# Routed rows sent to their expert's slots while the attention stage still runs, and PSUM banks exchanged between two uses

## The chip, the cores and the metric

The kernel runs on one core of one Trainium2 chip. The metric is the device time of one execution in microseconds (us), of which the median over several runs is taken. Engines are named as in the profile: PE is TensorE, DVE is VectorE, ACT is ScalarE, POOL is GpSimd, SP is SyncE, which here only issues DMAs.

## What is computed

The reference is one transformer layer with conditioning (adaLN). Its first half is attention within segments of 128 tokens, its second half a mixture of 16 experts with one expert per token and a capacity of 512 tokens per expert:

```python
B, L, D, H, E = 4, 2048, 512, 2048, 16        # 8192 tokens, 64 segments of 128
sa, ca, ga, sb, cb, gb = (silu(c) @ wmod) split in six rows per batch
h = layernorm(x) * (1 + ca) + sa
x = x + ga * attention(h)                      # softmax within each segment, plus a global row per segment
h = layernorm(x) * (1 + cb) + sb               # called h2 in the kernel
score = softmax(h @ Wg + bg); gate = max(score); idx = argmax(score)
pos  = rank of the token among those of its expert, in token order
keep = pos < 512
buf[idx, pos] = h          (kept tokens alone)
y = relu(buf @ W1[e] + b1[e]) @ W2[e] + b2[e]
x = x + gb * where(keep, y[idx, pos] * gate, 0)
```

## The kernel before

Each engine has a program written out by hand; semaphores connect them. There are three stages.

**Prologue.** The weights of attention are multiplied together and split in a high and a low part.

**Group stage.** The 8192 tokens are 16 groups of 512 rows (`GS` = 4 tiles of 128). Every engine has a function `iteration(i, ...)`, which is called once per turn; the turn of group i works on several groups at once: the projections of group i (`cur`), the softmax, the attention product and the second layer norm of group i-1 (`prev`), the router's logits of group i-2 (`prev2`) and the slots of group i-3 (`prev3`); `nxt` prepares group i+1. The order within a turn is the order of the code. On each engine the turns run in a hardware loop over pairs of groups, with the first and the last turns written out.

In a turn PE does: `g_tile` 0 and 1, transposes of `h2` of group i-2, `ranks`, `g_tile` 2, transposes of `prob` (L709), `g_tile` 3, the product with `u` of group i-1 (L323 to L726), the product that makes the next `u`, the router's partial logits (L742), the transposes of the normalised rows of group i+1 (`transpose_xn`, L593), the transposes of the partial logits (`logit_parts`, L754), and the scores (L762). `transpose_xn` writes the four banks of `big`; tile k waits until DVE has made `u_lo` of tile k (`u_split`). The scores go to a bank of their own, `s_bank`.

DVE first writes `prob`, then the statistics of the next group, then `pt_lo` (L1353), then `route_slots` (L1296 to L1326), then, tile by tile, `h2` (L1366, from PSUM) and `xr` (L1370, both inputs in SBUF), statistics, two tiles of `u_lo` (L1388), `query_const` (L1260), and two more tiles of `u_lo`.

POOL in a turn does `normalise1` of group i+1 (L1547 to L1557, in place in `xa`), the `scatter` of group i-3 (L1579), which writes 8 bytes for each token (its number and its gate) to the token's slot in `slot_table` in HBM, 4 indirect DMAs of 128 tokens, and then scales `h2` of group i-1 (L1600 and L1604, four tiles of each). SP stores `h2` to `h2_rows` in HBM in token order when it is ready (L449).

**Expert stage.** For each expert 4 blocks (`NB`) of 512 hidden units, all in PE time. The expert's 512 rows have to be in `xh`: the slot table is loaded (L489), DVE copies the token numbers of one expert to `tok_h`, and POOL gathers the rows from `h2_rows` with 4 indirect DMAs (`gather_h`, L1623). PE transposes them (L805), ACT and DVE split them in `bt_hi` and `bt_lo`, and `hidden` begins. `split_w1(n, ...)` on DVE (L1396 and L1398) makes the two parts of the n-th block of W1; PE's `hidden(n)` waits for it (`w1_split`). Later in an expert POOL gathers the residual rows `xo` and the rows `gb_rows`, and scatters the results (L1654).

The lines of the functions that the change touches:

## Time and profile before

| what | value |
|---|---|
| median of 3 runs | 1890.59 us (1890.21 to 1891.96) |
| time of the profiled execution | 1888.11 us |
| its span, first to last instruction | 1886.4 us, so 1.7 us lie around it |
| group stage, turns of about 36 us | from about 88 to 642 us |
| from the last score product to the first expert matmul | 626 to 691.4 us |
| expert stage | 691.4 us to the end |
| PE busy | 1797.0 us (95%) |
| DVE, ACT, POOL busy | 1224.1, 821.9, 868.4 us |

All rows are of one profiled execution, and their times count from its first instruction. A row of the timeline gives the start, the duration, the engine, the line, the operation with its output and inputs, and in square brackets how long the engine had been idle before it and who ended that. The busy time of PE is that of pipelined matmuls, so it tells where PE stands still, not how well it is used.

### The profile page before, as it was taken

To read this page: it belongs to the slowest core of one execution; us is meant where nothing else is said; L and a number is where in the kernel's file an instruction comes from. 1 tells how busy PE (TensorE), PEld (TensorE's weight loads), DVE (VectorE), ACT (ScalarE), POOL (GpSimd) and SP (SyncE) were. 2 spreads that over 40 slices of the span, in tenths; PEclk is the share of its full clock that TensorE was granted. 3 is DMA by queue.
4 is the path that set the end of the run, shared out by engine and by line. 5 is a ranking of instruction groups with operands and counts; after the bars stand their busy time and mean duration, and the time that the engine had idled before them with its cause. 6 is when DMAs were issued, how large, how long until landed. Compare 5 with 4: busy or idle time off the path is not lost.

```text
span 1886.4 us, 28121 instructions
## 1 busy us (share of the span) xinstructions
PE 1797.0 (95%) x9137; PEld 1487.0 (79%) x9138; DVE 1224.1 (65%) x1882; ACT 821.9 (44%) x1322; POOL 868.4 (46%) x709
## 2 busy tenths in 40 slices
PE   8999999999999549999999999998998999999998
PEld 3677787787787437889888888887888988888886
DVE  4568888888887754555554554537757886455762
ACT  2544554554544323434434343336445564334541
POOL 2145655655655441334343432416637756233632
PEclk9999999999999779999999999999999999999999
DMA  8422432332342424343535434345545455434622
GB/s 279 140 90 90 150 119 90 133 135 89 115 164 82 176 68 164 126 142 128 187 141 174 145 123 145 117 164 183 175 141 206 165 212 180 156 122 156 223 81 67
DMA packets 137915, 270.77 MB, mean 144 GB/s; under 512 B 17633, under 2 KB 18221, under 8 KB 137862
## 3 DMA queue, kind: packets, MB, share of 16 engines
q1 hardware_dynamic: 115338, 221.27, 33.5%
q0 software_dynamic: 22528, 48.86, 8.0%
q8 instruction: 29, 0.48, 0.1%
q14 instruction: 20, 0.16, 0.0%
HBM read 237.71 MB, written 50.72 MB: 153 GB/s over the span
## 4 chain that ended last, share of the span: by engine, by line
PE 77%; DVE 11%; issue 4%; ACT 3%; POOL 2%; DMA 2%; SPq 1%; DVEq 0%; POOLq 0%; ACTq 0%
PE bank L323 23%; PE bank L325 23%; PE bank L324 23%; PE bank L762 2%; PE bank L698 2%; DVE prob L1260 2%; DVE h L1366 1%; DVE stats L1145 1%; DVE xr L1370 1%; PE bank L805 1%; PE bank L593 1%; DVE u_lo L1388 1%; PE bank L582 1%; DVE ht_lo L1206 1%; DMA g_x<-in_L_attn_x_dram 1%
## 5 line engine op out<-in xcount | busy, mean ns | idle before, releaser
L1427 DVE TENSOR_TENSOR h_lo<-h_f,h_hi 128x512 fp32r<-128x512 f32 x256 | 221.3, 885 | 363.5 <-ACT h_f L1079 363.4
L1078 ACT ACTIVATE h_hi<-bank,b_col 128x512 fp32r<-128x512 f32 x256 | 176.4, 689 | 598.1 <-PE bank L325 582.7
L323 PE MATMUL bank<-bt_hi,w_hi 128*128 128x512 f32 (+4 forms) x1024 | 360.7, 352 | 9.4 <-DVE w_lo L1398 5.5
L324 PE MATMUL bank<-bt_lo,w_hi 128*128 128x512 f32 (+4 forms) x1024 | 359.3, 351 | 0.0
L325 PE MATMUL bank<-bt_hi,w_lo 128*128 128x512 f32 (+4 forms) x1024 | 359.2, 351 | 0.0
L323 PE MATMUL bank<-w_hi,h_hi 128*128 128x512 f32 x832 | 325.9, 392 | 2.8 <-issue 2.7
L324 PE MATMUL bank<-w_lo,h_hi 128*128 128x512 f32 x832 | 324.2, 390 | 0.0
L325 PE MATMUL bank<-w_hi,h_lo 128*128 128x512 f32 x832 | 324.0, 389 | 0.0
L323 PEld LDWEIGHTS bank<-bt_hi,w_hi 128*128 128x128 f32 x1024 | 194.5, 190 | 35.5 <-issue 9.3
L324 PEld LDWEIGHTS bank<-bt_lo,w_hi 128*128 128x128 f32 x1024 | 194.6, 190 | 21.0
L325 PEld LDWEIGHTS bank<-bt_hi,w_lo 128*128 128x128 f32 x1024 | 194.4, 190 | 20.3
L1623 POOL DMA_INDIRECT gb_rows<-mod_rows,tok_g x64 | 76.4, 1194 | 275.0 <-DVE tok_g L1504 221.2
L323 PEld LDWEIGHTS bank<-w_hi,h_hi 128*128 128x128 f32 x832 | 156.3, 188 | 35.6 <-issue 4.5
L325 PEld LDWEIGHTS bank<-w_hi,h_lo 128*128 128x128 f32 x832 | 156.2, 188 | 32.8
L324 PEld LDWEIGHTS bank<-w_lo,h_hi 128*128 128x128 f32 x832 | 156.3, 188 | 31.0
L1623 POOL DMA_INDIRECT xh<-h_rows,tok_h x64 | 87.3, 1364 | 201.4 <-DVE tok_h L1486 178.1
L1419 DVE TENSOR_TENSOR w_lo<-raw,w_hi 128x2048 fp32r<-128x2048 f32 x64 | 151.6, 2368 | 41.3 <-ACT w_hi L1068 41.3
L1079 ACT ACTIVATE h_f<-bank,b_col 128x512 f32<-128x512 f32 x256 | 174.3, 681 | 0.0
L1398 DVE TENSOR_TENSOR w_lo<-raw,w_hi 128x2048 fp32r<-128x2048 f32 x64 | 151.5, 2367 | 2.2
L1649 POOL TENSOR_TENSOR yo<-yo,gb_rows 128x512 f32<-128x512 f32 x60 | 98.5, 1642 | 108.8 <-DVE yo L1448 107.4
L1068 ACT ACTIVATE w_hi<-raw 128x2048 fp32r<-128x2048 f32 x64 | 122.6, 1916 | 0.0
L1654 POOL DMA_INDIRECT out_dram<-yo,tok_x x64 | 79.9, 1248 | 80.7 <-POOL yo L1651 53.9
(265 smaller groups left out, 3224.3 us busy)
## 6 DMA issues: line engine op xcount, KB each, us to landing
raw<-in_L_ffn_W_dram SPq DMA_DIRECT2D x128, 1024.0 KB, 5.5
xa<-in_L_attn_x_dram SPq DMA_DIRECT2D x16, 1024.0 KB, 5.3
xr<-in_L_attn_x_dram SPq DMA_DIRECT2D x16, 1024.0 KB, 8.0
out_dram<-xr SPq DMA_DIRECT2D x16, 1024.0 KB, 10.0
h_rows<-h SPq DMA_DIRECT2D x16, 1024.0 KB, 4.3
b_bc<-in_L_ffn_b_dram SPq DMA_DIRECT2D x16, 256.0 KB, 6.3
wm_a<-in_L_wmod_dram SPq DMA_DIRECT2D x2, 1024.0 KB, 11.1
wm_b<-in_L_wmod_dram SPq DMA_DIRECT2D x2, 1024.0 KB, 11.3
```

The costliest lines, as they stand in the source:

```text
L323: pe.matmul(o, a_hi, b_hi, start=start, stop=False)
L324: pe.matmul(o, a_hi, b_lo, start=False, stop=False)
L325: return pe.matmul(o, a_lo, b_hi, start=False, stop=stop)
L1068: act.activation(w2_hi[b % 2][:], raw[2 * (b % 2) + 1][:], ACT.Copy).then_inc(w2_hi_done, 1)
L1078: act.activation(h1_hi[b % 2][:, j, :], h_bank[j][:, :], ACT.Relu, bias=bias)
L1079: act.activation(h1_f[:, j, :], h_bank[j][:, :], ACT.Relu, bias=bias).then_inc(relu_done, 1)
L1398: dve.tensor_tensor(w1_lo[b % 2][:], raw[2 * (b % 2)][:], w1_hi[b % 2][:].bitcast(F32), ALU.subtract) \
L1419: dve.tensor_tensor(w2_lo[b % 2][:], raw[2 * (b % 2) + 1][:], w2_hi[b % 2][:].bitcast(F32), ALU.subtract) \
L1427: dve.tensor_tensor(h1_lo[b % 2][:, j, :], h1_f[:, j, :], h1_hi[b % 2][:, j, :].bitcast(F32), ALU.subtract) \
L1623: pool.indirect_dma_start(out=rows[:, j, :], out_offset=None, in_=source, in_offset=bass.IndirectOffsetOnAxis(tokens[:, j:j + 1], 0), boun ...
L1649: pool.tensor_tensor(yo[:, j, :], yo[:, j, :], gb_rows[:, j, :], ALU.mult).then_inc(y_scaled, 1)
L1654: pool.indirect_dma_start(out=out_rows, out_offset=bass.IndirectOffsetOnAxis(tok_x[:, j:j + 1], 0), in_=yo[:, j, :], in_offset=None, bound ...
```

## The change

There are three parts.

1. **Banks.** The scores now go to `big[3]` and tile 3 of `transpose_xn` to the bank that the scores had (`t1_last`). Tile 3 no longer waits for `u_split`; the scores do. The transposes of `logit_parts` move from the end of the turn to behind `g_tile` 0 of the next turn. On ACT, `empty_parts` moves behind `modulate`.
2. **Routed rows.** `h2_rows` in HBM is gone. SP clears a new tensor `slot_rows` (8192 rows of 2 KB, 16 MB) in four DMAs in the first two turns. In turn i, SP copies `h2` of group i-2 to a single SBUF buffer `stage` (L473), after the rows of group i-3 have left it. POOL sends the rows of `stage` to their slots with 4 indirect DMAs (`send_rows`), and behind them the 4 of the token table (`send_tokens`), at the end of its turn, behind the scaling of `h2`. DVE's first `h2` write of a turn waits for `h2_staged` in place of `h2_stored`. The last two groups are sent from `h2` directly.
3. **Experts.** SP loads `xh` with 4 plain DMAs (`load_xh`); `gather_h`, `tok_h` and the clearing of `xh` are gone. DVE's `rows_low(0)` moves ahead of the wait for the table, and `split_w1(0, 0, 0)` waits for the last rows.

```diff
+    def t1_bank(g, k):
+        return t1_last if k == KC - 1 and not (isinstance(g.n, int) and g.n == 0) else big[k]
...
 @block.sync
+        def clear_slots(quarter):
+            rows = slot_dram.rearrange("(q p a) d -> q p a d", q=4, p=P)[quarter]
+            sp.dma_start(rows, no_rows[:].unsqueeze(1).to_broadcast([P, E * CAP // P // 4, D])) \
+                .then_inc(slots_cleared, 16)
...
+            if prev2:
+                if isinstance(i.n, int) and i.n == 2:
+                    sp.wait_ge(slots_cleared, 16 * 4)
+                g, before = i.plus(-2), i.plus(-3)
+                if not isinstance(i.n, int) or i.n >= 3:
+                    sp.wait_ge(rows_sent[before.par], 16 * GS * (before.half + 1))
                 sp.wait_ge(h2_ready, 4 * g.n + 4)
-                sp.dma_start(group_rows(h2_dram, g), h2[g.par][:]).then_inc(h2_stored[g.par], 16)
+                stand_alone(sp, sp_passed)
+                sp.dma_start(stage[:], h2[g.par][:]).then_inc(h2_staged[g.par], 16)
...
         load_w1((0, 0), 0)
         load_w2((0, 0), 0)
         load_w1((0, 1), 1)
+        iteration(Group(NG // 2, 0), False, True, False, False)
+        sp.wait_ge(rows_sent[1], 16 * GS * (NG // 2 - 1))
         load_w2((0, 1), 1)
-        iteration(Group(NG // 2, 0), False, True, False)
-        sp.wait_ge(h2_ready, 4 * NG)
+        def load_xh(e):
+            rows = slot_dram[bass.ds(e * CAP, CAP), :].rearrange("(p j) d -> p j d", j=GS)
+            for j in range(GS - 1, -1, -1):
+                sp.dma_start(xh[:, j, :], rows[:, j, :]).then_inc(xh_in[j], 16)
+        for par in range(2):
+            sp.wait_ge(rows_sent[par], 16 * GS * (NG // 2))
+        load_xh(0)
         for par in range(2):
             sp.wait_ge(scattered[par], 16 * GS * (NG // 2))
...
+                if b == 0 and not last:
+                    sp.wait_ge(bt_full, 4 * e + 4)
+                    stand_alone(sp, sp_passed)
+                    load_xh(e + 1)
...
 @block.tensor
             for k in range(KC):
-                if not first:
+                if not first and k < KC - 1:
                     pe.wait_ge(u_split, 4 * g.n - 4 + k + 1)
...
                 g_tile(i, 0)
+            if prev3:
+                pe.wait_ge(parts_out, i.plus(-3).n + 1)
...
+                for s in range(GS):
+                    last = pe.transpose(pt_bank[:, chunk(s)], logit_parts[:, chunk(s)], ident[:])
+                last.then_inc(lg_full, 1)
+            if g_tiles:
                 g_tile(i, 1)
...
-            if prev2:
-                pe.wait_ge(parts_out, p2.n + 1)
...
             if cur:
                 pe.wait_ge(gt_done, 4 * n + 4)
+                pe.wait_ge(u_split, 4 * n + 4)
...
 @block.vector
-                    dve.wait_ge(h2_stored[p1.par], 16 * p1.half)
+                    dve.wait_ge(h2_staged[p1.par], 16 * p1.half)
...
-        dve.memset(xh[:], 0.0).then_inc(rows_cleared, 1)
+        dve.wait_ge(rows_sent[(NG - 1) % 2], 16 * GS * (NG // 2))
         split_w1(0, 0, 0)
-
+        rows_low(0)
         dve.wait_ge(table_in, 16)
...
 @block.gpsimd
+        def send_rows(g):
+            late = isinstance(g.n, int) and g.n >= NG - 2
             pool.wait_ge(route, RT * g.n + RT)
+            if late:
+                pool.wait_ge(h2_ready, 4 * g.n + 4)
+            else:
+                pool.wait_ge(h2_staged[g.par], 16 * (g.half + 1))
             stand_alone(pool, pool_passed)
+            rows = h2[g.par] if late else stage
+            for s in range(GS):
+                pool.indirect_dma_start(out=slot_dram, out_offset=bass.IndirectOffsetOnAxis(slot_i[g.par][:, s:s + 1], 0),
+                                        in_=rows[:, s, :], in_offset=None, bounds_check=E * CAP - 1,
+                                        oob_is_err=False).then_inc(rows_sent[g.par], 16)
...
-            if prev3:
-                scatter(i.plus(-3))
+            if prev3 and rows_first:
+                send_rows(i.plus(-3))
...
+            if prev3 and not rows_first:
+                send_rows(i.plus(-3))
+            if prev3:
+                for k in tokens:
+                    send_tokens(i.plus(k))
...
-        iteration(Group(NG // 2, 0), True, False, True)
-        iteration(Group(NG // 2, 1), False, False, True)
-        iteration(Group(NG // 2 + 1, 0), False, False, True)
+        iteration(Group(NG // 2, 0), True, False, True, rows_first=True)
+        iteration(Group(NG // 2, 1), False, False, True, ())
+        iteration(Group(NG // 2 + 1, 0), False, False, True, (-4, -3))
...
-        pool.wait_ge(rows_cleared, 1)
-        gather_h(0)
-        gather_h(1)
-        pool.wait_ge(rows_cleared, 3)
+        pool.wait_ge(rows_cleared, 2)
         gather_x(0)
         with pool.Fori(1, E - 1) as e:
-            gather_h(e + 1)
             finish_rows(e - 1)
```

POOL's program, second half of a loop turn of before, from `normalise1` to the scaling (`xa_99` and `h_0_110` are one of the two buffers of `xa` and `h2`):

```order
L1547 TENSOR_TENSOR per_tok<-per_tok,half_neg 128x4 [waits ln1_ready]
L1549 REGISTER_ALU
L1550 TENSOR_TENSOR per_tok<-per_tok 128x4 [waits ln1_rstd]
L1557 TENSOR_SCALAR xa_99<-xa_99,per_tok 128x512 [waits ln1_rstd]
L1557 TENSOR_SCALAR xa_99<-xa_99,per_tok 128x512 x3
L1576 ISA
L1579 DMA slot_table<-pay_83,slot_i_81 8192x2 [waits route]
L1579 DMA slot_table<-pay_83,slot_i_81 8192x2 x3
L1546 ISA
L1547 TENSOR_TENSOR per_tok<-per_tok,half_neg 128x4 [waits ln2_ready]
```

The same engine now, from the end of the scaling of one turn to `normalise1` of the next:

```order
L1663 TENSOR_TENSOR h_1_110<-h_1_110,sb_tab 128x512 [waits h2_scaled]
L1623 ISA
L1627 REGISTER_ALU [waits route]
L1631 DMA slot_rows<-stage,slot_i_82 8192x512 [waits h2_staged1]
L1631 DMA slot_rows<-stage,slot_i_82 8192x512 x3
L1638 DMA slot_table<-pay_84,slot_i_82 8192x2 x4
L1589 ISA
L1590 TENSOR_TENSOR per_tok<-per_tok,half_neg 128x4 [waits ln1_ready]
L1592 REGISTER_ALU
L1593 TENSOR_TENSOR per_tok<-per_tok 128x4 [waits ln1_rstd]
L1600 TENSOR_SCALAR xa_98<-xa_98,per_tok 128x512 [waits ln1_rstd]
```

Where 4 sends stood between `normalise1` and the scaling, 8 now stand between the scaling and the next turn's `normalise1`.

DVE's program behind the last group, before (`w_hi_160` is the first block of W1, `w_hi_162` the second):

```order
L1456 CAST expert_rows<-bank 1x16 [waits count_full]
L1457 MEMSET xh 128x2048
L1396 CAST w_hi_160<-raw_156 128x2048 [waits w1_in0]
L1463 COPY tok_h<-table 128x4 [waits table_in]
...
L1433 TENSOR_TENSOR bt_lo<-bank,bt_hi 128x512 [waits bt_hi_done] x3
L1476 MEMSET xo 128x2048
L1477 MEMSET gb_rows 128x2048
...
L1396 CAST w_hi_162<-raw_158 128x2048 [waits w1_in1]
```

and now (`w_hi_161` the first block, `w_hi_163` the second):

```order
L1446 CAST w_hi_161<-raw_157 128x2048 [waits w1_in0,rows_sent1]
L1448 TENSOR_TENSOR w_lo_162<-raw_157,w_hi_161 128x2048 [waits w1_hi_done]
L1483 TENSOR_TENSOR bt_lo<-bank,bt_hi 128x512 [waits bt_hi_done] x4
L1513 CAST tok_f<-table 128x64 [waits table_in]
...
L1524 MEMSET xo 128x2048 [waits index_step]
L1525 MEMSET gb_rows 128x2048
L1477 TENSOR_TENSOR h_lo_174<-h_f,h_hi_173 128x512 [waits relu_done]
L1446 CAST w_hi_163<-raw_159 128x2048 [waits w1_in1]
L1448 TENSOR_TENSOR w_lo_164<-raw_159,w_hi_163 128x2048 [waits w1_hi_done]
```

The wait for the table stood ahead of the rows of expert 0 (`bt_lo`); it now stands behind them, and the second block of W1 is behind it still.

## Rows read from the trace of the kernel before

**Rows 1.** Windows: us, then busy us (instructions) of PE, PEld, DVE, ACT, POOL, clock, DMA share, GB/s

```profile
400.00:500.00 100.00, 97.75 (x558) 78.68 (x556) 85.36 (x199) 52.64 (x103) 61.56 (x56) 1.00 0.36 126
```

**Rows 2.** Timeline of PE in two turns of the loop

```profile
478.75 1.25 PE L593 MATMUL bank<-ident,xa 128*128 128x128 f32 x8 [0.57 <-DVE u_lo L1388]
...
494.06 0.60 PE L709 MATMUL bank<-ident,prob 128*128 128x128 f32 x4
...
514.95 1.25 PE L593 MATMUL bank<-ident,xa 128*128 128x128 f32 x8 [0.90 <-DVE u_lo L1388]
```

**Rows 3.** Timeline of DVE in the same turns

```profile
463.10 0.69 DVE L1366 TENSOR_TENSOR h<-bank,ga_tab 128x512 f32<-128x512 f32 x1
...
495.47 0.69 DVE L1353 TENSOR_TENSOR pt_lo<-bank,pt_hi 128x512 fp32r<-128x512 f32 x1 [2.29 <-ACT pt_hi L1028]
...
499.48 0.69 DVE L1366 TENSOR_TENSOR h<-bank,ga_tab 128x512 f32<-128x512 f32 x1 [0.30 <-PE bank L726]
...
514.22 1.27 DVE L1388 TENSOR_TENSOR u_lo<-bank,u_hi 128x512 fp32r<-128x512 f32 x2
```

**Rows 4.** Timeline of POOL in the same turns

```profile
486.50 1.29 POOL L1604 TENSOR_TENSOR h<-h,sb_tab 128x512 f32<-128x512 f32 x1 [0.18 <-POOL h L1600]
493.25 1.02 POOL L1547 TENSOR_TENSOR per_tok<-per_tok,half_neg 128x4 f32<-128x4 f32 x1 [5.46 <-DVE per_tok L1152]
...
494.77 3.07 POOL L1557 TENSOR_SCALAR xa<-xa,per_tok 128x512 f32<-128x512 f32 x4 [0.21 <-POOL per_tok L1550]
```

**Rows 5.** Timeline of DVE and of POOL in the first turn

```profile
81.85 0.69 DVE L1260 SCALAR_TENSOR_TENSOR prob<-xa,vc_tab 128x512 f32<-128x512 f32 x1
...
82.59 1.14 DVE L1260 SCALAR_TENSOR_TENSOR prob<-xa,vc_tab 128x512 f32<-128x512 f32 x1
...
82.08 4.22 POOL L1557 TENSOR_SCALAR xa<-xa,per_tok 128x512 f32<-128x512 f32 x4 [0.21 <-POOL per_tok L1550]
```

**Rows 6.** Landing: the last 4 scatters of result rows (L1654); the page's `h2` stores

```profile
DMA to landing us min/median/max: 2.7/2.7/2.8
...
h_rows<-h SPq DMA_DIRECT2D x16, 1024.0 KB, 4.3
```

**Rows 7.** Timeline of DVE in the last two turns and behind them

```profile
603.30 0.69 DVE L1353 TENSOR_TENSOR pt_lo<-bank,pt_hi 128x512 fp32r<-128x512 f32 x1 [5.45 <-ACT pt_hi L1028]
...
606.30 0.69 DVE L1366 TENSOR_TENSOR h<-bank,ga_tab 128x512 f32<-128x512 f32 x1 [0.16 <-PE bank L726]
...
638.15 0.69 DVE L1366 TENSOR_TENSOR h<-bank,ga_tab 128x512 f32<-128x512 f32 x1 [0.15 <-PE bank L726]
...
666.73 0.14 DVE L1326 COPY pay<-tokids 128x4 int32<-128x4 int32 x1
...
680.39 0.17 DVE L1463 COPY tok_h<-table 128x4 int32<-128x4 int32 x1 [7.45 <-DMA table<-slot_table]
...
693.50 1.76 DVE L1476 MEMSET xo<- 128x2048 f32 x1 [0.38 <-issue]
...
699.18 2.29 DVE L1398 TENSOR_TENSOR w_lo<-raw,w_hi 128x2048 fp32r<-128x2048 f32 x1
```

**Rows 8.** Timeline of POOL in the last turns

```profile
628.36 1.26 POOL L1604 TENSOR_TENSOR h<-h,sb_tab 128x512 f32<-128x512 f32 x1 [0.18 <-POOL h L1600]
...
667.72 3.74 POOL L1579 DMA_INDIRECT slot_table<-pay,slot_i  x1 [0.49 <-issue]
...
675.36 0.97 POOL L1579 DMA_INDIRECT slot_table<-pay,slot_i  x1 [0.30 <-issue]
```

**Rows 9.** Timeline of SP and PE between the stages

```profile
677.51 0.37 SPq L489 DMA_DIRECT2D table<-slot_table  x1
...
689.42 1.02 PE L805 MATMUL bank<-ident,xh 128*128 128x128 f32 x4 [0.26 <-DMA xh<-h_rows,tok_h]
691.38 0.50 PE L323 MATMUL bank<-bt_hi,w_hi 128*128 128x512 f32 x1 [0.93 <-DVE bt_lo L1433]
...
702.42 0.39 PE L323 MATMUL bank<-bt_hi,w_hi 128*128 128x512 f32 x1
```

More of the change, by code:

```diff
@@ L177, in build_block @@
     h2t, = over(r_h2t, ("h2t", full, F32))
+    stage, = over(r_raw0, ("stage", full, F32))
     seg_sq = [P, GS, P]
@@ L180, in build_block @@
     logit_parts, = over(cursor[0], ("logit_parts", [P, ROWS], F32))
+    no_rows, = over(r_raw0, ("no_rows", [P, D], F32))
     batch_rows = [P, NBATCH, D]
@@ L210, in build_block @@
     QCS2 = [QC, QCS]
-    raw = over(r_raw0, ("raw0", full, F32)) + over(r_xa, ("raw1", full, F32), ("raw2", full, F32)) \
-        + over(r_ht, ("raw3", full, F32))
+    raw = over(r_xa, ("raw0", full, F32), ("raw1", full, F32)) + over(r_ht, ("raw2", full, F32)) \
+        + over(r_raw0, ("raw3", full, F32))
     w1_hi, w1_lo, w2_hi, w2_lo = [None] * 2, [None] * 2, [None] * 2, [None] * 2
@@ L280, in build_block @@
     x2_stored = [sem(f"x2_stored{i}") for i in range(2)]
-    h2_stored = [sem(f"h2_stored{i}") for i in range(2)]
+    h2_staged = [sem(f"h2_staged{i}") for i in range(2)]
     h2t_full, h2t_done, parts_full, parts_out, lg_full = (sem(k) for k in (
@@ L696, in iteration @@
                         pe.wait_ge(gt_done, 4 * n + k - 1)
+                    if prev and big[(k + 2) % 4] is s_bank:
+                        pe.wait_ge(exp_done, 4 * p1.n + 4)
                     for s in range(GS):
@@ L744, in iteration @@
                 last.then_inc(parts_full, 1)
+            if cur and not g_tiles:
+                pe.wait_ge(pro_evac, PRO_END)
             if nxt:
                 transpose_xn(i.plus(1), False)
-            if prev2:
-                pe.wait_ge(parts_out, p2.n + 1)
-                if prev:
-                    pe.wait_ge(pt_split, p1.n + 1)
-                stand_alone(pe, pe_passed)
-                wait_past(pe, lg_step, p2.n)
-                for s in range(GS):
-                    last = pe.transpose(pt_bank[:, chunk(s)], logit_parts[:, chunk(s)], ident[:])
-                last.then_inc(lg_full, 1)
             if cur:
-                if not g_tiles:
-                    pe.wait_ge(pro_evac, PRO_END)
                 pe.wait_ge(gt_done, 4 * n + 4)
+                pe.wait_ge(u_split, 4 * n + 4)
                 for s in range(GS):
@@ L945, in modulate @@
                 for rows in (ht_hi, ht[g.par]):
-                    ins = act.activation(rows[:, k, :], big[k][:, :], ACT.Identity,
+                    ins = act.activation(rows[:, k, :], t1_bank(g, k)[:, :], ACT.Identity,
                                          bias=mod_col[:, 0, k, bass.ds(batch_of(g), 1)],
@@ L1045, in iteration @@
                 normalise2(3)
+            if nxt:
+                modulate(i.plus(1))
             if prev2 and cur:
                 empty_parts()
-            if nxt:
-                modulate(i.plus(1))
         iteration(Group(0, 0), True, False, False, True, False)
@@ L1481, in expert @@
                 n = NB * e + b
-                if b == 0 and not last:
-                    for j in range(GS):
-                        dve.wait_ge(xh_in[j], 16 * (e + 1))
-                    stand_alone(dve, dve_passed)
-                    dve.tensor_copy(tok_h[:], tok[:, bass.ds(GS * (e + 1), GS), 0]).then_inc(tok_h_ready, 1)
                 split_hidden(e, b, 0)
@@ L1562, in _ @@
         inverse_root(0, gsum_stats, gsum_rstd, VE2, MN2, RS2, NR2, NSEG, 1)
+        pool.wait_ge(pro_evac, GROWS + 1)
+        pool.wait_ge(v_split, KC)
+        pool.memset(no_rows[:], 0.0).then_inc(no_rows_made, 1)
         pool.wait_ge(pro_evac, SG + 1)
```

54 lines of the change are left out of this document (31 added, 23 removed).

## The prediction

> **What bounds the kernel now.** I read the windows first: of 100 us in the loop of groups PE stands still for 2.25 [rows 1]. The timeline then shows the one large hole, between the last scores of the group stage and the first expert matmul at 691.38 [rows 9]. From there PE works almost without a gap (the expert stage is 1195 of the 1886.4 us of the span), so nothing that is saved on the other engines there shortens the time. Two places are left: the turns of the group stage, and the hole.
>
> A turn of the loop. The timelines show a ring of two engines. PE stands still only ahead of the third tile of the transposes of `xa`, until DVE has made `u_lo` of that tile: 0.57 and 0.90 us in two successive turns [rows 2]. I call t the start of DVE's first `h2` write of a turn (L1366): 463.10 and 499.48 [rows 3]. From t to that `u_lo` are 514.22 + 0.64 - 499.48 = 15.4 us, all DVE work. From there PE needs 494.06 - 478.75 = 15.3 us to the transposes of `prob` [rows 2], and from those to the next t are 499.48 - 494.06 = 5.4 us over ACT and DVE. 15.4 + 15.3 + 5.4 = 36.1. From 463.10 to 606.30 are four turns [rows 3, 7], 35.8 each, and that mean I use.
>
> The hole. Between the last group's `pay` (666.73 + 0.14 [rows 7]) and the first expert matmul stand POOL's last table sends, the last of which starts at 675.36 [rows 8], the load of the table at 677.51, the gather of `xh`, whose last tile PE transposes at 689.42, and 2.0 us of splitting [rows 9].
>
> **Banks.** PE's third tile keeps its wait; only the fourth loses one, and its `u_lo` is ready 0.64 us behind the third's, half of the 1.27 for two [rows 3], about the time of PE's own tile (1.25 for two [rows 2]). The transposes of `logit_parts` stay between the same two points of the ring. I take 0 (bounds: 0 to -0.1 a turn).
>
> **Clearing.** 16 MB in two halves, each between two turns' loads. In the loop DMA has a share of 0.36 at 126 GB/s [rows 1], so about 350 GB/s when full: 8.4 MB take 24 us, and some 23 of 36 us are free. It just fits; I take 0. If a half ran at the 1.05 MB in 4.3 us of a store of `h2` [rows 6], 34 us, the next rows of x would come up to 11 us later than now, and the turn's prefetch would hide part of that.
>
> **The sends on POOL.** POOL ends the scaling 24.7 us after t (486.50 + 1.29 - 463.10 [rows 3, 4]), and is idle 5.46 us before `normalise1` at 493.25 [rows 4]. Now 8 sends stand there, at 0.97 + 0.30 = 1.27 us each [rows 8], 10.2 us. So `normalise1` begins 4.8 us later or more, and its four operations on `xa`, which began 1.5 us behind its start and took 3.07, beside `route_slots` [rows 4], fall from 24.7 + 0.3 + 10.2 + 1.5 = 36.7 us after t on, beside the next turn's L1366 and L1370. PE needs `xa` some 15 us later than that, so the delay itself costs nothing. Two things follow.
>
> First, `route_slots` becomes free of a neighbour. From `pt_lo` to t it takes 4.0 us in the loop [rows 3], and 3.0 us in a turn without `normalise1` [rows 7]. With half of the turns nearer to 3.5, the ring of DVE and PE loses about 0.75, to 35.05 us.
>
> Second, L1370, which reads two tiles from SBUF, now meets `xa`. The first turn shows such a meeting: L1260, also with two SBUF inputs, takes 1.14 instead of 0.69 us beside `xa`, and the four POOL operations 4.22 [rows 5] instead of 3.07. Two of the four L1370, which are 1.3 us apart, fall into those 3 to 4 us for certain: I take c = 2 x 0.45 = 0.9 us (bounds 0 and 1.8, four hits). The Trainium skill has a rule on this, in SBUF — State Buffer, Who interferes with whom: a DVE instruction with two SBUF inputs and a GpSimd one that reads SBUF exclude each other for a whole instruction. By that, a hit costs up to a whole operation on `xa`, 0.77 us, and four hits 3.1 us a turn instead of 0.9.
>
> **The new ring over `stage`.** There is one `stage`, so SP can copy group i-2 only when the rows of i-3 have landed, these are sent only behind the scaling of i-1, and DVE's first write for group i waits for that copy. Behind SP's waiting copy stands nothing urgent: the next load of x comes at the turn's end. From t: the scaling ends at 24.7; 0.3 to the first send; the fourth starts 3.8 later; it lands 2.7 later, as the result rows of the same size do [rows 6]; 0.1 for SP; 4.3 for a 1 MB copy, as the store of `h2` [rows 6]; 0.1 for DVE. Sum 36.0 us, about a turn of now, but c lies inside it as well. So a turn takes the larger of 35.05 + c and 36.0 + c: 36.9 us. Eleven turns have both: 11 x (36.9 - 35.8) = 12.1.
>
> The last turn (606.30 to 638.15, 31.85 us [rows 7]) I count with the hole: the copy of group 13 is ready at 628.36 + 1.26 [rows 8] + 0.3 + 3.8 + 2.7 + 0.1 + 4.3 + 0.1 = 640.9, so the tail shifts by 2.8 us.
>
> **The hole, now.** In times of the old trace plus that shift: the last `pay` is ready at 669.7; the rows of group 15 are sent from 670.0 to 674.9 and land at 676.6; the four loads of `xh`, together 1 MB, take 4.3 us as the store [rows 6] and 0.6 for the four issues, to 681.5. The first `hidden` can start 2.0 us later, at 683.5: 7.9 us earlier than now. It takes 702.42 - 691.38 = 11.0 us [rows 9], to 694.5. But the second one waits for `split_w1(1)`, whose place on DVE is behind the wait for the token table, and the table now comes later: behind the rows, 8 table sends run from 675.2 to 685.4, plus what the DVE casts take from them. Such a meeting is in the trace: a send of 3.74 us beside a memset and a cast [rows 8]. With 2.5 us for it and 2.15 from the last send's start (675.36) to the load of the table (677.51), that load is issued at 688.8 and used 2.9 later (680.39 - 677.51 [rows 7, 9]), at 691.7. Then six small operations, 1.5 us by estimate from that copy's 0.17 and the waits between them, and 699.18 + 2.29 - 693.50 = 8.0 us from the memset of `xo` to the end of `w_lo` [rows 7], with 0.4 ahead: 701.6. Before, the second `hidden` began at 702.42. So the hole gives 0.8 us in spite of the 7.9 (bounds: 3.6 without the shift, -2 if the sends meet more). The 64 gathers that POOL loses lay beside PE's full time; if they came back into view, it would be as `split_w1(1)` above.
>
> **Sum.** 12.1 - 0.8 = 11.3 us. Against the profiled execution's 1888.1 us that is 1899.4; the median of the runs is 2.5 above it, so 1901.9.
>
> **Rivals.** A, the forecast, a turn of 36.4 to 37.3 us: 1896 to 1907, chance 0.50.
> B, both new costs stay small, and it gets faster: c is near 0 because `normalise1` slips between the L1370, and the copy within SBUF lands a us sooner than a store to HBM. Then a turn takes 35.05 us, 11 x 0.75 = 8.3 less, and the tail shift falls to 1.8 us, so the hole gives 1.8: 1880.5. It decides from a ring over `stage` under 35.8 us with c. For it speak the 5.46 us of idle POOL [rows 4] and `route_slots`; against it [rows 5]. Chance 0.20. The skill's DMA: Bandwidth & Descriptors, Anatomy of one DMA, says that most of a DMA's fixed cost is the write receipt, heaviest for HBM; no row here copies within SBUF, and by it the copy would take less than 4.3.
> C, the two cancel (a ring of 35.7 to 35.9 with c): 0 from the turns, -0.8 from the hole, 1887 to 1893. Chance 0.12.
> D, the sends or the copy land late, since four sends of 256 KB follow each other at 1.27 us: 1.5 us more per turn and 1.5 in the tail give 18 on top of A: 1920. Against it: result rows that land in 2.7. Chance 0.12.
> E, the clears delay x in the first turns by 5 to 9 us on top of A: 1907 to 1911. Chance 0.06.
>
> **How the numbers follow.** The forecast is A's, 1901.9. The range holds A, C and E and reaches into B and D, 1882 to 1916. A change under 0.2%, 3.8 us, is about what a measurement of this kernel cannot tell from none. Faster: B and a little of C, 0.22. Same: most of C and A's lower edge, 0.12. Slower: the rest, 0.66.
>
> **What the profile after would show.** Right: DVE's first L1366 of each turn waits for the copy to `stage`; two L1370 of a turn near 1.1 us; turns of about 36.9; `pt_lo` to the last `pay` shorter; between the first and the second `hidden` a PE gap of about 7 us that ends with `w_lo`. Wrong: turns under 36, or no gap there. A wait for `xa` in the first three turns would be E.

## The result, and the profile after

The changed kernel takes 1906.54 us (median of 5 runs, 1906.14 to 1911.90) against 1890.59; the ratio is 1.0091 with a 95% interval of 1.0080 to 1.0103. It is slower by some 16 us. One of the five executions of the kernel before took 6576 us, unlike any other of it, and is left out of the ratio. The profiled execution is one of the longer ones: span 1909.0 us, against 1886.4 before, so 22.6 us are to be found in the two traces.

I cut both traces at two points: t, the start of DVE's first `h2` write of a turn, and the first `hidden` matmul of the experts. A `hidden` matmul is the first layer of an expert.

| | twelve turns, the 4th t to the 16th | 16th t to the first `hidden` | first `hidden` to the end |
|---|---|---|---|
| before | 638.15 - 211.78 = 426.4 | 691.38 - 638.15 = 53.2 | 1195.0 |
| after | 654.59 - 211.80 = 442.8 | 700.39 - 654.59 = 45.8 | 1208.6 |
| difference | +16.4 | -7.4 | +13.6 |

**The turns.** The page of the profile has this row for DVE's `h2` write (busy us, mean ns, then the idle time ahead of it and what ended it):

```profile
L1416 DVE TENSOR_TENSOR h<-bank,ga_tab 128x512 f32<-128x512 f32 x64 | 43.7, 682 | 22.8 <-DMA stage<-h 14.8 <-PE bank L783 8.0
```

DVE now waits 14.8 us for the copy to `stage`, which no row of before names. One turn in the timelines of DVE, POOL and SP shows the ring:

```profile
541.25 0.69 DVE L1403 TENSOR_TENSOR pt_lo<-bank,pt_hi 128x512 fp32r<-128x512 f32 x1 [2.20 <-ACT pt_hi L1077]
...
544.18 0.20 DVE L1376 COPY pay<-tokids 128x4 int32 x1
545.73 0.69 DVE L1416 TENSOR_TENSOR h<-bank,ga_tab 128x512 f32<-128x512 f32 x1 [1.34 <-DMA stage<-h]
...
568.75 1.29 POOL L1663 TENSOR_TENSOR h<-h,sb_tab 128x512 f32<-128x512 f32 x1 [0.18 <-POOL h L1659]
570.21 1.07 POOL L1631 DMA_INDIRECT slot_rows<-stage,slot_i  x1 [0.17 <-DVE lg L1326]
...
574.64 0.98 POOL L1631 DMA_INDIRECT slot_rows<-stage,slot_i  x1 [0.30 <-issue]
...
577.28 0.48 SPq L473 DMA_DIRECT2D stage<-h  x1
...
582.25 0.69 DVE L1416 TENSOR_TENSOR h<-bank,ga_tab 128x512 f32<-128x512 f32 x1 [1.51 <-DMA stage<-h]
```

Read it from t = 545.73: the scaling ends at 570.04 (24.3 us later), the fourth row send starts at 574.64, the copy is issued at 577.28, and 4.97 us behind that DVE starts again: 36.5 us. The other ring, of DVE and PE, was ready 1.34 us earlier at the first of the two t, and 1.51 us at the second. Its tail, from `pt_lo` to the end of `pay`, is 544.18 + 0.20 - 541.25 = 3.1 us. In the kernel before, `pay` ends at 463.05 and at 499.17, 3.5 and 3.7 us behind the start of `pt_lo`: `route_slots` has lost its neighbour.

Five of the turns are like this one, 36.5 to 36.7 us. The six from 285.05 to 509.12 are longer, 36.85 to 38.0 us, and in three of these (from 285.05, 359.84 and 434.69) DVE doesn't wait for the copy at all. Here is the first of the three, by DVE, PE and a window (its columns are named below):

```profile
288.44 1.14 DVE L1420 TENSOR_TENSOR xr<-xr,h 128x512 f32<-128x512 f32 x1
...
300.96 1.94 PE L636 MATMUL bank<-ident,xa 128*128 128x128 f32 x8 [1.85 <-DVE u_lo L1438]
...
301.00:304.40 3.40, 3.40 (x16) 3.40 (x17) 3.29 (x4) 3.36 (x6) 3.22 (x3) 0.50 0.93 307
...
322.12 0.22 DVE L1376 COPY pay<-tokids 128x4 int32 x1
322.34 0.69 DVE L1416 TENSOR_TENSOR h<-bank,ga_tab 128x512 f32<-128x512 f32 x1
```

One write of `xr` takes 1.14 instead of 0.69 us beside GpSimd's `xa`, `u_lo` comes about that much later, and PE stands still for 1.85 us ahead of its third tile (1.28 to 1.54 in the five turns). Then the granted clock is 0.50 for 3.4 us, PE ends this stretch another 1.6 us later, and `pay` is ready only at t: here the ring of DVE and PE is the longer one. The other two have an `xr` of 1.18 and 1.14 us, waits of 2.03 and 1.95 us, and the same fall of the clock. No such fall is in the loop turns of the kernel before, where that wait is 1.11 us at most. This chain is read from the trace; no run has it alone.

**Between the stages** (timeline of PE, then of DVE):

```profile
695.97 3.65 PE L854 MATMUL bank<-ident,xh 128*128 128x128 f32 x16 [12.04 <-DMA xh<-slot_rows]
700.39 0.80 PE L331 MATMUL bank<-bt_hi,w_hi 128*128 128x512 f32 x1 [0.77 <-DVE bt_lo L1483]
...
718.60 0.79 PE L331 MATMUL bank<-bt_hi,w_hi 128*128 128x512 f32 x1 [5.46 <-DVE w_lo L1448]
...
734.67 0.79 PE L331 MATMUL bank<-w_hi,h_hi 128*128 128x512 f32 x1 [2.25 <-DVE h_lo L1477]
...
683.48 0.14 DVE L1376 COPY pay<-tokids 128x4 int32<-128x4 int32 x1
...
692.11 1.23 DVE L1446 CAST w_hi<-raw 128x2048 fp32r<-128x2048 f32 x1 [7.97 <-DMA slot_rows<-h,slot_i]
...
708.48 0.20 DVE L1513 CAST tok_f<-table 128x64 f32<-128x64 int32 x1 [6.35 <-DMA table<-slot_table]
...
712.54 1.76 DVE L1525 MEMSET gb_rows<- 128x2048 f32 x1 [0.37 <-issue]
...
716.02 2.29 DVE L1448 TENSOR_TENSOR w_lo<-raw,w_hi 128x2048 fp32r<-128x2048 f32 x1
```

The first `hidden` starts 7.4 us earlier behind the last t than in [rows 9], and the second, at 718.60, is 64.0 us behind it, against 64.3 before. It waits for `w_lo`, which stands on DVE behind the token table (708.48), the indices and two memsets.

**Behind that** TensorE runs part of the time at the lower of its two clocks. Windows of after (us, then busy us (instructions) of PE, PEld, DVE, ACT, POOL, clock, DMA share, GB/s):

```profile
676.00:696.00 20.00, 2.44 (x19) 1.04 (x19) 9.39 (x37) 0.89 (x3) 12.68 (x12) 0.59 0.23 66
...
700.40:713.20 12.80, 12.74 (x48) 10.11 (x48) 5.41 (x11) 4.48 (x8) 1.95 (x2) 0.87 0.40 110
...
718.60:734.70 16.10, 13.86 (x49) 10.88 (x49) 9.82 (x10) 5.94 (x9) 0.00 (x0) 0.82 0.57 196
```

and, within them, the three stretches at the lower clock:

```profile
700.40:703.80 3.40, 3.40 (x8) 2.72 (x9) 1.73 (x3) 0.68 (x2) 1.95 (x2) 0.50 0.02 1
717.50:724.30 6.80, 5.70 (x13) 4.46 (x14) 4.81 (x5) 0.08 (x1) 0.00 (x0) 0.50 0.11 15
734.50:737.90 3.40, 3.23 (x8) 2.56 (x9) 2.29 (x2) 1.13 (x1) 0.00 (x0) 0.50 0.02 5
```

and of the kernel before, the same two stretches of work:

```profile
691.40:702.40 11.00, 11.00 (x48) 9.10 (x49) 10.21 (x11) 4.40 (x8) 3.75 (x2) 1.00 0.03 8
702.40:715.50 13.10, 11.06 (x49) 8.82 (x47) 9.09 (x9) 8.65 (x12) 2.00 (x2) 1.00 0.65 219
```

A granted clock of 0.5 is 1.2 GHz, 1.0 is 2.4 GHz; a value between them is the mean of a window that holds both. PE is busy for 3.40 + 5.70 + 3.23 = 12.3 us at the lower clock here, and not at all in the kernel before from 691.4 to 1437. By estimate half of this, 6.2 us, is what the lower clock costs. The same 48 matmuls take 12.7 us instead of 11.0, and the stretch behind the second `hidden` 16.1 instead of 13.1, with about as long a wait inside it.

### The profile page after: what moved, and what is told of

It reads as the page before. It is cut to its first block, busy times and chain, and to the rows that moved or that the text cites. A ratio compares the mean times of both kernels' runs of the same rounds, so it can differ in the third digit from the quotient of the medians.

```text
span 1909.0 us, 28241 instructions
## 1 busy us (share of the span) xinstructions
PE 1805.8 (95%) x9137; PEld 1496.1 (78%) x9138; DVE 1215.4 (64%) x1865; ACT 822.5 (43%) x1322; POOL 858.5 (45%) x710
## 4 chain that ended last, share of the span: by engine, by line
PE 75%; DVE 10%; issue 5%; DMA 4%; POOL 3%; ACT 2%; POOLq 0%; DVEq 0%; ACTq 0%; SPq 0%
PE bank L331 23%; PE bank L332 22%; PE bank L333 22%; DMA stage<-h 2%; PE bank L811 2%; DVE h L1416 1%; DVE xr L1420 1%; DVE stats L1194 1%; DVE prob L1309 1%; DMA slot_rows<-stage,slot_i 1%; PE bank L854 1%; PE bank L636 1%; POOL h L1659 1%; PE bank L753 1%; PE bank L625 1%
## 5 line engine op out<-in xcount | busy, mean ns | idle before, releaser
L331 PE MATMUL bank<-bt_hi,w_hi 128*128 128x512 f32 (+4 forms) x1024 | 363.2, 355 | 13.3 <-DVE w_lo L1448 12.1
L331 PEld LDWEIGHTS bank<-bt_hi,w_hi 128*128 128x128 f32 x1024 | 196.1, 192 | 40.0 <-issue 14.8
L333 PEld LDWEIGHTS bank<-bt_hi,w_lo 128*128 128x128 f32 x1024 | 196.2, 192 | 20.8
L331 PEld LDWEIGHTS bank<-w_hi,h_hi 128*128 128x128 f32 x832 | 156.7, 188 | 36.5 <-issue 5.1
L1117 ACT ACTIVATE w_hi<-raw 128x2048 fp32r<-128x2048 f32 x64 | 122.6, 1916 | 0.0
L331 PE MATMUL bank<-ht_hi,m_hi 128*128 128x512 f32 x256 | 106.2, 415 | 2.2 <-DVE ht_lo L1255 2.2
## 6 DMA issues: line engine op xcount, KB each, us to landing
slot_rows<-no_rows SPq DMA_DIRECT2D x4, 4096.0 KB, 25.1
```

The costliest lines, as they stand in the source:

```text
L331: pe.matmul(o, a_hi, b_hi, start=start, stop=False)
L333: return pe.matmul(o, a_lo, b_hi, start=False, stop=stop)
L1117: act.activation(w2_hi[b % 2][:], raw[2 * (b % 2) + 1][:], ACT.Copy).then_inc(w2_hi_done, 1)
```

## The experiments

All have the changed kernel as their base, but for the two that start from the kernel before. The table comes first, since each run is read in the same three pieces; what an edit doesn't touch should agree between rows. The first three columns are of the profiled execution, the last is the median of all runs of that kernel. The kernel before, measured again beside them, had medians of 1890.5 to 1891.6.

| run | edit | 12 turns | to first `hidden` | to the end | median us |
|---|---|---|---|---|---|
| before | | 426.4 | 53.2 | 1195.0 | 1890.6 |
| after | | 442.8 | 45.8 | 1208.6 | 1906.5 |
| r4 | before + banks | 424.7 | 52.5 | 1197.1 | 1891.2 |
| r1 | rows early | 429.1 | 45.7 | 1208.7 | 1895.0 |
| r2 | tokens early | 438.1 | 45.4 | 1206.3 | 1904.5 |
| r3 | table late | 445.2 | 45.8 | 1200.6 | 1908.5 |
| r8 | the same again | 445.4 | 45.8 | 1196.4 | 1902.1 |
| r5 | r1 + late `normalise1` | 444.4 | 45.2 | 1207.4 | 1912.2 |
| r6 | r5 + table late | 444.3 | 45.5 | 1197.2 | 1903.7 |
| r7 | before + late `normalise1` | 443.2 | 54.0 | 1197.6 | 1912.5 |
| r15 | rows behind the root | 467.9 | 46.0 | 1207.8 | 1936.3 |
| r16 | r15 + table late | 468.0 | 45.6 | 1196.7 | 1928.6 |
| r17 | clears doubled | 446.1 | 45.9 | 1205.3 | 1940.9 |
| r18 | `stage` in halves + table late | 425.2 | 46.9 | 1198.4 | 1885.7 |

**Banks alone (r4).** The ten pieces of the diff that deal with `big`, `s_bank`, `t1_last`, the transposes of `logit_parts` and ACT's order, put into the kernel before.

> The kernel before with the exchange of the banks alone (with it the transposes of logit_parts earlier in PE's turn and ACT's order at the turn's end); rows stored and gathered as before. Theory (banks cost nothing): 1890.6 within 2 us, turns of 35.8. Rival (the earlier transposes of logit_parts make PE wait for ACT inside the ring, or the freed fourth tile gives time): a turn changes by 0.2 to 0.6 us, 3 to 9 us in all.

Measured: 1891.15, ratio 0.9991 (0.9982 to 1.0000). Eleven turns from the fourth t take 395.0 us against 394.5, only the last is 2.2 us shorter. Banks cost nothing, as forecast.

**Who sends when (r1, r2).** In r1 the rows go out between `normalise1` and the scaling and the tokens behind the scaling; in r2 it is the other way round. Both have four sends at either place.

```diff
-        def iteration(i, prev, nxt, prev3, tokens=(-3,), rows_first=False):
+        def iteration(i, prev, nxt, prev3, tokens=(-3,), rows_first=True):
```

> In every turn the four row sends stand between normalise1 and the scaling, in the 5.5 us in which GpSimd was idle there, and the four token sends behind the scaling. Theory (the ring over stage sets the turn): the copy to stage can then be issued some 12 us after DVE's first h2 write instead of 31, no first h2 write waits for it, turns go back to 35.8 us, the last one starts at about 638 to 640 instead of 654.6, and the time falls by 15 to 16 us, to 1890 to 1892. Rival (the eight sends as such, or their traffic, make the turn longer): turns stay above 36.3 and at least 8 of the 16 us stay.

> The same, the other way round: token sends between normalise1 and the scaling, row sends behind the scaling. GpSimd has four sends at either place, as in the run with early rows. Ring over stage: the rows leave at the same time as in the changed kernel, so turns stay at 36.5 us or more with waits for the copy to stage, 1904 to 1908. Rival (normalise1 that comes late beside DVE's work): normalise1 comes as early as in the kernel before, so turns of 35.8 and 1890 to 1893.

r1: 1895.02, ratio 1.0019 (1.0010 to 1.0027). 11.5 us of the 16 are gone, and with them every wait for the copy; the twelve turns are 429.1 us. r2: 1904.49, as expected, and DVE still waits for the copy, though GpSimd's load is the same. So it is the place of the row sends, not their number or `normalise1`, that costs: the ring over `stage` holds. r1 was expected at 35.8 us a turn and 1890 to 1892 and has 36.2 to 36.5 in most turns, so it comes out 3 us above. The timelines of DVE and POOL in r1 show why: `normalise1` is beside `route_slots` again, and costs more there than in the kernel before.

```profile
532.01 1.04 POOL L1590 TENSOR_TENSOR per_tok<-per_tok,half_neg 128x4 f32<-128x4 f32 x1
...
533.54 3.05 POOL L1600 TENSOR_SCALAR xa<-xa,per_tok 128x512 f32<-128x512 f32 x4 [0.21 <-POOL per_tok L1593]
...
534.11 0.69 DVE L1403 TENSOR_TENSOR pt_lo<-bank,pt_hi 128x512 fp32r<-128x512 f32 x1 [2.21 <-ACT pt_hi L1077]
...
535.22 0.64 DVE L1350 TENSOR_SCALAR per_tok<-per_tok 128x4 f32<-128x4 f32 x1
...
535.89 0.70 DVE L1354 SCALAR_TENSOR_TENSOR per_tok<-per_tok 128x4 f32<-128x4 f32 x1
...
538.25 0.69 DVE L1416 TENSOR_TENSOR h<-bank,ga_tab 128x512 f32<-128x512 f32 x1
```

From `pt_lo` to the end of `pay` it is 4.1 us here and in seven more turns, against 3.4 to 3.9 in the turns of the kernel before. Two operations on 128x4 take 0.64 and 0.70 us, which in the changed kernel took 0.17 and 0.16; in the kernel before, one or two of them take about 0.5 us in most turns.

**The table work on DVE later (r3, r8).** The wait for the table, the indices and both memsets move behind `w2_low` of the first block.

```diff
                 w2_low(n, b)
+                if b == 0 and first:
+                    read_table()
```

> DVE waits for the token table, makes the indices and clears xo and gb_rows only behind the second half of block 0's w2 split, not ahead of the first expert's first block. Theory: the gap of 5.46 us ahead of the second hidden goes, and with it the 2.2 us gap behind it and some of the stretch at the lower TensorE clock: 6 to 10 us less, 1897 to 1901. Rival (the gap only moves to the next split, since DVE has the same work): 0 to 2 us less.

> The kernel with the late table work once more, unchanged, since its first six runs lay between 1900 and 1927 and its profile had one turn of 40.8 us that no other kernel shows. If that spread was chance: a median of 1897 to 1901, 6 to 9 us under the changed kernel. If it belongs to the edit: the spread and a median above 1905 come again.

The profile agrees in both: the gap ahead of the second `hidden` is gone, and from the first `hidden` to the third piece of work there are 26.5 us (r3) instead of 34.3.

```profile
704.63 0.80 PE L331 MATMUL bank<-bt_hi,w_hi 128*128 128x512 f32 x1 [0.77 <-DVE bt_lo L1483]
731.13 0.49 PE L331 MATMUL bank<-w_hi,h_hi 128*128 128x512 f32 x1 [2.64 <-issue]
```

In the table the last piece is 8 to 12 us shorter. The whole time is less clear: r3 gave 1908.5 with runs from 1900 to 1927, r8, the same kernel, 1902.1 (1900.6 to 1905.4). So the second run found 4.4 us of the 6 to 9 expected, and the first none. The turns ahead of the edit differ too: the twelve take 445.2 and 445.4 us instead of 442.8, and ahead of the last turn the granted clock falls to 0.50, as above, in one turn of r3 and five of r8. r3's profile has one turn of 40.8 us. In it the clock is at 0.50 for 3.4 us from 230.6 on, and ACT starts its third `gt` 3.5 us behind the last matmul of `g_tile` 2 (which ends at 246.59; in the changed kernel's turn shown above ACT comes 0.04 us behind it):

```profile
250.05 0.69 ACT L1003 ACTIVATE gt<-bank,u_col 128x512 f32<-128x512 f32 x1 [4.48 <-PE bank L333]
```

r17 has such a turn too (41.7 us, with the clock at 0.50 for 3.4 us as well). What holds ACT there stays open. This and the falls of the clock may be why the times of these kernels spread more than those of the kernel before, but no run shows that.

**`normalise1` kept away from `route_slots` (r5, r6, r7).** The changed kernel had shown 3.1 us for `route_slots` alone. I tried to get that without the ring over `stage`, by a wait ahead of `normalise1`; in r7 that is the only edit to the kernel before.

```diff
+            if nxt and prev3:
+                pool.wait_ge(route, RT * i.plus(-3).n + RT)
             if nxt:
                 normalise1(i.plus(1))
```

> The kernel with early rows, and GpSimd waits for the slots of group i-3 (route) ahead of normalise1, so that normalise1 doesn't run beside DVE's route_slots. Theory: two rings stand behind the changed kernel's turn; the one over stage is gone with the early rows, and the ring of DVE and PE is 35.2 us when route_slots has no neighbour (36.5 less the 1.34 us wait for the copy, in the changed kernel), against 36.4 in the run with early rows. So turns of 35.2 and 11 to 14 us less than with early rows alone: 1881 to 1884. Rival (xa that comes later, beside DVE's first writes, gives the time back): turns of 36 or more, 1891 to 1896.

> Early rows, the late normalise1 and the late table work together. If the three are independent: 8 us less than the run without the late table work, 1873 to 1877. If the gap at the second hidden was short already (3.56 us with early rows): 3 to 6 us less, 1877 to 1880.

> The kernel before, with nothing but that wait for route ahead of normalise1. Theory (route_slots beside normalise1 costs DVE 0.5 to 1 us a turn, whatever the rows do): turns of 35.1 instead of 35.8, 6 to 9 us faster, 1882 to 1885. Rival (the gain needs the banks exchanged, or is eaten by a later xa): within 2 us of the kernel before.

All three expectations were off by 24 to 31 us, and their rivals as well: measured 1912.2, 1903.7 and 1912.5. `route_slots` did lose its neighbour, but the turns became 37.2 to 37.8 us, in r7 up to 38.2. The timelines of POOL and ACT in r7 name the link I had left out:

```profile
521.99 1.06 POOL L1579 DMA_INDIRECT slot_table<-pay,slot_i  x1 [0.17 <-issue]
...
525.89 1.39 POOL L1579 DMA_INDIRECT slot_table<-pay,slot_i  x1 [0.30 <-issue]
527.30 1.51 POOL L1547 TENSOR_TENSOR per_tok<-per_tok,half_neg 128x4 f32<-128x4 f32 x1
...
529.13 2.22 ACT L1005 ACTIVATE h<-xr,per_tok 128x512 f32<-128x512 f32 x3 [2.32 <-POOL per_tok L1550]
531.26 0.57 ACT L998 ACTIVATE u_hi<-bank 128x512 fp32r<-128x512 f32 x1
```

`normalise1` can start only at t (515.66 in this turn), the sends follow it, and only then comes the second inverse root (L1547), which ACT's scaling of `h` waits for; behind `h` on ACT's queue stands the `u_hi` that `u_lo` is made from. ACT's `h` starts 529.13 - 515.66 = 13.5 us behind t, in the kernel before 10.6 to 10.9. So there is a third ring, from t through `normalise1`, the sends and the inverse root on GpSimd to ACT and DVE, and with `normalise1` tied to t it becomes the longest. In the changed kernel nothing stands between `normalise1` and that root, so a late `normalise1` did no harm there: ACT's `h` starts 10.6 to 11.2 us behind t. This is read from the timelines; r15 puts the root straight behind `normalise1` and has 10.6 again, but changes more than that.

**Rows behind the inverse root (r15, r16).** The rest of the idea: root first, then rows, scaling, tokens, and no added wait.

```diff
                 inverse_root(p1.n, ln2_ready, ln2_rstd, VE2, MN2, RS2, NR2)
+                if prev3 and not rows_first:
+                    send_rows(i.plus(-3))
```

> GpSimd's turn in the order normalise1, inverse root, row sends, scaling, token sends; no added wait. Theory, as corrected by the two runs with the wait: what they lost was the inverse root that ACT's h (and behind it u_hi and ht) waits for, put off by the sends that followed the late normalise1; the root must come straight behind normalise1. Then the rows leave 11 us into the turn (no ring over stage), the scaling ends near 29 us, the tokens near 34, and normalise1 starts when route_slots is nearly over: turns of 35.2 to 35.6, so 9 to 14 us less than with early rows alone (1895.0): 1881 to 1886. Rival (h2 that is ready 4 us later, or the traffic, makes another wait): turns of 36 or more, 1891 and above.

> The same order together with the late table work on DVE. If the two add up: 4 to 9 us less than the run with the rows behind the root, 1874 to 1880. If the table comes early enough there: within 2 us of it.

Measured: 1936.25 and 1928.62, the slowest order of all, turns of 39.0 to 39.7 us. Both are some 50 us above what was expected, and the rival of r15, that a later `h2` makes another wait, is what came. The waits of PE (us in total, times, longest) show the cause: the scaled `h2` is wanted in the same turn, a few us behind the scaling's end, and now comes 1.2 to 2.4 us late in every turn. I had taken it for wanted a turn later.

```profile
PE bank L753 <- POOL h L1665: 28.4, 13, 8.2
PE bank L331 <- DVE ht_lo L1255: 14.6, 22, 0.7
```

r16 lies 7.6 us below r15: here the late table work gives what was expected of it.

**Clears doubled (r17).** Each clear is issued a second time, to a tensor that nothing reads.

> The changed kernel with every clear issued a second time to a tensor of its own that nothing reads: 33.5 MB instead of 16.8. Theory (the clears of the changed kernel just fit between the loads of x: 8.4 MB at 410 GB/s take 20.5 us and end about 3 us before the next load): the second half is in the way of the loads of x of groups 2 and 3, 17 us late each, of which the prefetch hides some; 10 to 30 us slower than the changed kernel. Rival (the loads get their share of the DMA engines beside the clears, and the prefetch hides the rest): within 3 us of it.

Measured: 1940.93, 34 us above the changed kernel and a little more than the 30 expected at most. In the profile it is 26.4, and 26.3 are lost ahead of the fourth t, where DVE waits 27.1 us for loads of `xa` (the twelve turns in the table take 3.3 us more than in the changed kernel, with the long one named above among them, and the last piece 3.3 less). The second and third t come at 147.76 and 201.11 instead of 139.06 and 175.25. The changed kernel's clears just fit: SP's next load of `xa` is issued at 117.22 there and at 117.13 before. Twice as many don't.

**`stage` in halves (r18).** GpSimd's order is that of the changed kernel. The copy is cut in two, each half with semaphores of its own, and DVE waits for a half only where it overwrites it. (To have semaphores for it, the clears use two of the prologue's.) The late table work is in as well.

```diff
-                if not isinstance(i.n, int) or i.n >= 3:
-                    sp.wait_ge(rows_sent[before.par], 16 * GS * (before.half + 1))
-                sp.wait_ge(h2_ready, 4 * g.n + 4)
-                stand_alone(sp, sp_passed)
-                sp.dma_start(stage[:], h2[g.par][:]).then_inc(h2_staged[g.par], 16)
+                for k in range(2):
+                    if not isinstance(i.n, int) or i.n >= 3:
+                        sp.wait_ge(rows_sent[before.par][k], 32 * (before.half + 1))
+                    sp.wait_ge(h2_ready, 4 * g.n + 4)
+                    stand_alone(sp, sp_passed)
+                    sp.dma_start(stage[:, 2 * k:2 * k + 2, :], h2[g.par][:, 2 * k:2 * k + 2, :]) \
+                        .then_inc(h2_staged[k], 16)
...
                 for s in range(GS):
 
+                    if s % 2 == 0 and (not isinstance(n, int) or n >= 3):
+                        dve.wait_ge(h2_staged[s // 2], 16 * p1.n - 16)
                     dve.wait_ge(av_full, 4 * p1.n + s + 1)
```

> The changed kernel with GpSimd's order as it is, but the copy to stage in two halves of 0.5 MB with semaphores of their own: the first half is copied when the first two row sends have landed, and DVE's first h2 write waits for that half alone, the third for the other. With it the late table work. Theory (the ring over stage sets the changed kernel's turn, one order of GpSimd's instructions is as good as it gets, and behind that ring stands the one of DVE and PE): the wait for the copy, 1.3 to 1.7 us a turn, goes, since the first half is ready some 4 us earlier and the second is wanted 2.7 us later; turns of 35.2 to 35.6, the last one starts near 633 to 637 instead of 654.6, and with 4 to 8 us for the table 1878 to 1886. Rival (the turns are held up by the traffic of eight sends and the copy, in whatever pieces): turns stay above 36.3 and the time is that of the late table work alone, 1899 to 1905.

Measured: 1885.71 (11 runs), ratio to the kernel before 0.9977 (0.9968 to 0.9986): faster than both kernels, by 4.8 us than the one before measured beside it and by 20.8 than the changed one. By the table, what it gains on the kernel before lies between the last t and the first `hidden` (46.9 instead of 53.2 us). The page's row (its wait for the copy is 0.9 us in all), and one turn of DVE:

```profile
L1420 DVE TENSOR_TENSOR h<-bank,ga_tab 128x512 f32<-128x512 f32 x64 | 43.7, 683 | 7.5 <-PE bank L786 4.6 <-issue 1.3 <-DMA stage<-h 0.9
```

```profile
497.88 0.69 DVE L1420 TENSOR_TENSOR h<-bank,ga_tab 128x512 f32<-128x512 f32 x1 [0.31 <-issue]
...
499.94 0.95 DVE L1424 TENSOR_TENSOR xr<-xr,h 128x512 f32<-128x512 f32 x1
...
533.55 0.69 DVE L1420 TENSOR_TENSOR h<-bank,ga_tab 128x512 f32<-128x512 f32 x1
```

The ring over `stage` is open, with all eight sends where they were. The rival (traffic of sends and copy) falls: here are the same bytes in more pieces. Turns are 35.7 and 36.0 us, not the 35.2 to 35.6 expected, and as long as in the kernel before. About 0.3 us of the difference to 35.2 is the meeting of DVE's `xr` write with GpSimd's `xa` (0.95 instead of 0.69 us above), which had been hidden as long as DVE came 1.3 us later; from `pt_lo` to the end of `pay` it is 3.2 us instead of 2.9 to 3.15, which may be the second wait for the row sends in `route_slots`; the rest is open. PE's wait ahead of the third tile is 0.74 us at most, and the granted clock falls in none of the eleven turns: some 5 of the 17.6 us that the twelve turns gain on the changed kernel's are that, by estimate.

## Why the prediction was right, and where its sum was not

It forecast slower, 1901.9 us with 1882 to 1916 around it; measured are 1906.5. The mechanism is rival A, the forecast: the ring over the one `stage` takes the place of the ring of DVE and PE, and r1, r2 and r18 show it. That the turns' total came out is luck in part, and the expert stage behind the second `hidden` was left out. Going through its steps:

- **Banks**, 0: r4 measures 0.
- **Clearing**, 0 and just fitting: the loads of x keep their times, and r17 shows the edge. The page has 25.1 us from issue to landing for a clear; the 10.7 and 12.0 us in which SP's queue was busy with two of them at a time didn't reach the next load.
- **The ring over `stage`**, 36.0 + c = 36.9 us in each of eleven turns: measured 407.0 / 11 = 37.0, against 35.9 before. The total is right by luck, since its terms are not. c, the meeting of DVE's `xr` write with `xa`, was put at 0.9 in every turn, with two writes near 1.1 us; by the page's means it is 4 x (0.722 - 0.694) = 0.1 us a turn, and writes of 1.14 to 1.18 us stand in three turns alone, one in each. The chain of the copy was put at 36.0 and five turns take 36.5 to 36.7: 4.4 instead of 3.8 us to the fourth send (one of four took 1.48), and 5.0 instead of 4.4 from the copy's issue to DVE. That gives about 8 of the 12.5 us. The other 4.5 lie in the six turns from 285.05 to 509.12, 37.3 on average. Three of them are set by the ring of DVE and PE with the granted clock at 0.50 for 3.4 us, a term that the sum didn't have, and two of the three are followed by a turn in which the scaling ends 25.1 instead of 24.3 to 24.5 us behind t.
- **What lies behind that ring**, 35.05 us with `route_slots` free: the tail is 3.1 us as forecast, and the turns less their waits, 36.6 - 1.34 and 36.5 - 1.51, are 35.3 and 35.0. r18 shows that opening the first ring doesn't give it, since c comes back.
- **The last turn**, +2.8: measured 35.8 - 31.85 = 3.9, with a wait for the copy of

```profile
654.59 0.69 DVE L1416 TENSOR_TENSOR h<-bank,ga_tab 128x512 f32<-128x512 f32 x1 [4.96 <-DMA stage<-h]
```

- **The hole**: counted from the last t, the prediction had the first `hidden` 10.7 us earlier than before and the second 3.6 (it gives 7.9 and 0.8 with its shift of 2.8 taken in). Measured: 7.4 and 0.3. What stops the gain is what it named: the second waits for `split_w1(1)` behind the token table, with a gap of 5.5 us, forecast as about 7; r3, r8 and r18 take the gap away by moving the table work. The sizes were each a little short: the rows of group 15 land 692.11 - 683.62 = 8.5 us behind the last `pay` instead of 6.9, from there to the first `hidden` it is 8.3 instead of 6.9, and the table is used 24.9 us behind `pay` instead of 22.0.
- **What the sum left out**: 1190.4 - 1184.0 = 6.4 us behind the second `hidden`. The prediction took PE's work there as unchanged. It took 3.0 us more up to 734.67, and 1.9 more up to the transposes of the next expert's `xh` (788.43, in the kernel before 767.39); the last 1.5 are spread over the rest, where the clock is at 0.50 for 10.2 us (from 1331.9 and 1461.6) against 6.8 (from 1437.7). PE is busy there at the lower clock for 5.70 + 3.23 = 8.9 us, which by estimate costs half, 4.5 of the 6.4 us. In all runs with the table late the last piece of the table above is 1196 to 1201 us, in the others with the changed order 1205 to 1209. r3 and r8, which are one kernel, differ in it by 4.2 us: behind the first `hidden` the granted clock is 0.50 for 3.9 and 3.4 us in r3 and up to 790 never in r8, 3.6 us by the same estimate. So of the 13.6 us by which that piece is longer than before, 5.5 are the gap and some 6, by estimate, the clock.

So 12.1 + 2.8 - 3.6 = 11.3 us became 12.5 + 3.9 - 0.3 + 6.4 = 22.5 in the profiled execution, and 16 in the median. The profiled execution lies with the two longer of the five runs (1910.8 and 1911.9). Their mean granted clock is 0.977, that of the other three 0.979 to 0.981, so they spent more time at the lower clock; which falls of it they had beyond the others no trace shows.

The prediction weighed two rules. By the Trainium skill's SBUF — State Buffer, Who interferes with whom, a DVE write of `xr` and an operation on `xa` would shut each other out for whole operations; from this the prediction worked out up to 3.1 us a turn. The trace shows less: 29 of the 64 writes ran beside `xa`, with a median of 0.71 us and 1.18 at most, and 0.69 where they didn't. GpSimd lost more: its `xa` operations have a median of 1.27 us beside an `xr` write and 0.78 otherwise. By the Trainium skill's DMA: Bandwidth & Descriptors, Anatomy of one DMA, most of the fixed cost of a DMA that GpSimd issues is the write receipt, and it is heaviest for HBM; so the copy within SBUF would land sooner than the store to HBM of the same size. The copy, which SP issues, landed after 4.6 us (median), the store after 4.3 [rows 6]. Neither would have made the forecast better.

## What to carry to other kernels

A buffer in the middle of a pipeline makes a ring of its own: count it from the buffer's last reader through the copy to the writer that waits, against the turn, before anything is put behind it on a queue. Cutting such a copy in halves with a semaphore each may open the ring without more memory (here 17.6 us over twelve turns, some 5 of them by way of the clock). A wait of PE that grows by half a us can cost more than itself, when the granted clock falls behind it. And an engine's idle stretch is no free place: four orders of the same instructions on GpSimd gave 1895 to 1936 us, since its turn is a chain of short deadlines (the inverse root for ACT, the scaled `h2` for PE, `normalise1` clear of `route_slots`), each with a few us of slack at most.
